# A conditional residual block in fp32r halves: later expert transpose, later layer-0 start, another product order in fc2

## What is computed

```
x = x + (einsum('bsd,bdh->bsh', x, W[cat]) + b[cat])            # 512 -> 512, W[cat] of each entry
h = gelu(einsum('bnd,hd->bnh', x, fc1_w) + fc1_b)               # 512 -> 2048
shared = einsum('bnh,sh->bns', h, fc2_w) + fc2_b                # 2048 -> 384
expert = einsum('bnh,bph->bnp', h, experts_w[e]) + experts_b[e] # 2048 -> 128
x = x + concatenate([shared, expert], axis=-1)
```

## Time and profile before

| what | value |
|---|---|
| median of 3 runs | 1680.94 us (1680.47 to 1681.73) |
| the profiled execution's own time | 1681.4 us |
| its span | 1679.6 us |
| PE busy | 1639.4 us (98%), 7065 matmuls |
| PE weight loads busy | 1315.8 us (78%), beside the matmuls |
| DVE busy | 1176.4 us (70%) |
| ACT busy | 551.9 us (33%) |
| POOL busy | 195.1 us (12%) |
| mean granted PE clock | 0.997 |
| memory traffic | 144 GB/s over the span |

### The profile page before, as it was taken

One profiled execution on the slowest core, in us unless ns is written; L12 is line 12 of the kernel. 1 busy time (PEld: TensorE's weight loads), 2 busy tenths in 40 slices (PEclk: granted clock), 3 DMA queues, 4 the chain that ended last, 5 costly groups with the idle time before them and its releaser, 6 DMA issues.

```text
span 1679.6 us, 28015 instructions
## 1 busy us (share of the span) xinstructions
PE 1639.4 (98%) x7065; PEld 1315.8 (78%) x7065; DVE 1176.4 (70%) x2004; ACT 551.9 (33%) x927; POOL 195.1 (12%) x195
## 2 busy tenths in 40 slices
PE   7899999999999999999999999999999999999999
PEld 5778887877878778787877878778787787878887
DVE  5677667776777767776776677767777677767754
ACT  4343333333323333333332333333333333333321
POOL 0200100111020010200102001110200102001110
PEclk9999999999999999999999999999999999999999
DMA  7886776757677575775767767686775757757630
GB/s 207 185 190 150 147 149 147 156 129 162 127 163 151 131 156 118 167 159 133 149 133 160 156 144 157 131 157 135 163 153 131 155 118 164 163 131 151 134 61 26
DMA packets 884826, 243.44 MB, mean 145 GB/s; under 512 B 803688, under 2 KB 818168, under 8 KB 884732
## 3 DMA queue, kind: packets, MB, share of 16 engines
q1 hardware_dynamic: 740732, 203.75, 57.1%
q10 hardware_dynamic: 144000, 38.82, 10.7%
HBM read 209.93 MB, written 32.51 MB: 144 GB/s over the span
## 4 chain that ended last, share of the span: by engine, by line
PE 66%; SPq 20%; issue 8%; DMA 3%; DVE 2%; ACT 1%; DVEq 0%
PE ps_out L814 30%; PE ps_h L799 14%; PE ps_e L799 13%; PE ps_y L786 8%; SPq L386 8%; SPq L341 4%; SPq L320 2%; DMA e_blocks<-in_L_cond_experts_w 2%; SPq L399 2%; SPq L351 1%; SPq L393 1%; PE ps_t L745 1%; DVE e_whole L643 1%; DVE h L599 1%; DVE w2e L599 1%
## 5 line engine op out<-in xcount | busy, mean ns | idle before, releaser
L814 PE MATMUL ps_out<-w2e,h 128*128 128x512 f32 x3072 | 758.0, 396 | 10.0 <-DVE h L599 10.0
L814 PEld LDWEIGHTS ps_out<-w2e,h 128*128 128x128 f32 x3072 | 574.3, 188 | 152.5 <-DVE h L599 15.9
L799 PE MATMUL ps_e<-y_t,w 128*128 128x512 f32 x1536 | 376.8, 395 | 1.4 <-DVE y_t L599 1.4
L799 PE MATMUL ps_h<-y_t,w 128*128 128x512 f32 x1536 | 375.7, 394 | 0.0
L799 PEld LDWEIGHTS ps_e<-y_t,w 128*128 128x128 f32 x1536 | 290.7, 189 | 66.9 <-DVE y_t L599 1.6
L799 PEld LDWEIGHTS ps_h<-y_t,w 128*128 128x128 f32 x1536 | 288.5, 188 | 65.7
L643 DVE STREAM_TRANSPOSE e_whole<-e_blocks 128x512 f32<-128x512 f32 x256 | 182.0, 711 | 109.3 <-DMA e_blocks<-in_L_cond_experts_w 100.9
L530 ACT CAST w2e<-e_whole 128x512 fp32r<-128x512 f32 x256 | 158.6, 620 | 284.4 <-PE ps_out L814 157.4
L463 POOL TENSOR_TENSOR x_raw<-x_raw,b_all 128x512 f32<-128x512 f32 x60 | 85.3, 1422 | 1354.9 <-DMA x_raw<-in_x 1303.2
L499 ACT CAST w_split<-w_raw 128x512 fp32r<-128x512 f32 x244 | 145.7, 619 | 243.7 <-DMA w_raw<-in_L_cond_W 174.4
L599 DVE TENSOR_TENSOR w_split<-w_raw,w_split 128x512 fp32r<-128x512 f32 x244 | 161.1, 688 | 84.6 <-ACT w_split L499 83.7
(11 more groups left out here) (71 smaller groups left out, 431.3 us busy)
## 6 DMA issues: line engine op xcount, KB each, us to landing
e_blocks<-in_L_cond_experts_w SPq DMA_DIRECT2D x1024, 64.0 KB, 2.9
w_raw<-in_L_cond_W SPq DMA_DIRECT2D x248, 256.0 KB, 2.9
out<-resid SPq DMA_DIRECT2D x64, 256.0 KB, 4.7
x_blocks<-in_x SPq DMA_DIRECT2D x240, 64.0 KB, 2.4
b_all<-in_L_cond_b SPq DMA_DIRECT2D x60, 256.0 KB, 4.3
x_raw<-in_x SPq DMA_DIRECT2D x60, 256.0 KB, 4.6
y_rows<-y ACTq DMA_DIRECT2D x60, 256.0 KB, 2.8
x_blocks<-y_rows ACTq DMA_DIRECT2D x240, 64.0 KB, 3.7
```

The lines of the kernel that those rows point to most:

```text
L799: last = nc.tensor.matmul(h_bank(c)[:, :], w1[:, w, k, c * P:(c + 1) * P], y_t[:, a, k, :, :].rearrange("p b s -> p (b s)"), start=(k == 0 ...
L814: last = nc.tensor.matmul(ps_out[b][:, :], h[:, c % 2, a, b * S:(b + 1) * S], fc2_columns(c, c % 2, w, b), start=(c == 0 and n == 0), stop ...
```

## The change

Five edits, in the order of the diff:

1. L0_STEPS begins with 2 in place of 1: the first two slices of layer 0 for the next group are worked in step 2.
2. In `load_l0_in` everything that belongs to those two slices (two weight slices, the bias, x of entry 0) is issued in step 1 in place of step 0, and the x blocks of entry 1 and the third and fourth slices in step 2 in place of step 1. The x blocks of entry 0 stay in step 0.
3. In SP's step 0 the four stores come behind the expert loads of that step. In group 0 the loads of the two output biases move from step 0 to step 1.
4. On DVE `turn_next_e` stands behind `h_low` in every step, and not in step 0 alone. `turn_x` for entry 0 moves from step 0 to step 1.
5. On PE the three products in fc2 are taken as high-high, low-high, high-low (half of h first), which were high-high, high-low, low-high; and in step 0 of group 0 the first `turn_prep` comes ahead of fc1.

```
-    L0_STEPS = (1, 3, 5, 7, 9, 10, 11, 12)
+    L0_STEPS = (2, 3, 5, 7, 9, 10, 11, 12)
...
-                for b, step in ((0, 0), (1, 1), (2, L0_STEPS[1] + 3), (3, L0_STEPS[3] + 3)):
+                for b, step in ((0, 0), (1, L0_STEPS[0]), (2, L0_STEPS[1] + 3), (3, L0_STEPS[3] + 3)):
                     if c == step:
                         load_x_blocks(G, b)
                 for p in range(2 * GB):
-                    if c == (0 if p == 0 else L0_STEPS[p - 1]):
+                    if c == (L0_STEPS[0] - 1 if p == 0 else L0_STEPS[p - 1]):
...
                 for b in range(GB):
-                    if c == (0 if b == 0 else L0_STEPS[2 * b - 1] + 1):
+                    if c == (L0_STEPS[0] - 1 if b == 0 else L0_STEPS[2 * b - 1] + 1):
                         load_b0(G, b, load_l0_in.cat)
                         load_x(G, b)
...
                     if more:
                         load_l0_in(g + 1, c)
-                    if c == 0 and not first(g):
-                        store(g - 1)
...
                         load_experts(g + 1, quad - NC // QUAD, next_idx, [b])
-                    if first(g) and c == 0:
+                    if c == 0 and not first(g):
+                        store(g - 1)
+                    if first(g) and c == 1:
                         sp.dma_start(b2_all[:, :], fc2_b.rearrange("(o n) -> o n", o=1).to_broadcast([P, SHARED]))\
...
-                    if c > 0:
-                        turn_next_e(g, c, more)
                     h_high(g, c)
                     prep_low(prep_in_step(g, c, 0))
                     h_low(g, c)
-                    if c == 0:
-                        turn_next_e(g, c, more)
+                    turn_next_e(g, c, more)
                     prep_low(prep_in_step(g, c, 1))
                     if more:
-                        if c == 0:
+                        if c == L0_STEPS[0] - 1:
                             turn_x(g + 1, 0)
...
-                    for n, (a, w) in enumerate(((0, 0), (0, 1), (1, 0))):
+                    for n, (a, w) in enumerate(((0, 0), (1, 0), (0, 1))):
                         last = nc.tensor.matmul(ps_out[b][:, :], h[:, c % 2, a, b * S:(b + 1) * S],
...
                 for c in range(NC):
+                    if c == 0:
+                        turn_prep(prep_in_step(g, c, 0))
                     fc1(g, c)
-                    turn_prep(prep_in_step(g, c, 0))
+                    if c > 0:
+                        turn_prep(prep_in_step(g, c, 0))
```

## The result

The changed kernel takes 1740.44 us, the median of 4 runs (1736.18 to 1741.76), against 1681.18 for the kernel before: a ratio of 1.035, 95% interval 1.033 to 1.037. It is slower by 59 us, where 73 were forecast; the time lies inside the range of 1716 to 1767. The profiled execution took 1740.58 us, its span 1738.8.

A forecast was written before the change was run, and what follows sets the result against it. PE bounds the kernel, busy 1639.4 us of a 1679.6 us span. The terms -10 + 53 + 2 + 34 - 6 = +73 us on 1681.4 gave a forecast of 1754 us, range 1716 to 1767.

The forecast's parts named there:

- The chain through SP: SP's queue to layer 0's first slices: 9.7 us delay against 5.6 us room, +53 us in 13 groups, +2 in group 1.
- the eight issues: Four expert blocks and four stores ahead of the first weight slice in SP's queue: 6.3 us of delay.
- the later start of the queue: SP's queue waits for the step-14 expert transpose, now behind h_low, so it starts each next group 3.4 us later.
- The clock: Slow matmuls behind the layer-0 stall at half clock: 2.6 us in each of 13 groups, +34 us.
- the second pair of slices: Third and fourth layer-0 slices, one step behind, meet a late PE: counted 0, up to 0.5 us a group for the range.
- The 10 us at h: fc2's wait for h's low half goes, since h no longer stands behind a waiting expert transpose: -10 us.
- Group 0: The 3.40 us stall in step 3 and its slow clock go: -3.4 - 2.6 = -6 us.
- The order of fc2's products: Same matmuls and weight loads in fc2 in either order: 0, bounded by 6 us either way.
- The faster rival: SP's queue absorbs the delay, layer 0 finds its slices ready, kernel gets faster: 1655 us, chance 0.11.
- the step of 5.6 us: PE reaches layer 0's first slices two blocks later, which gains 5.6 us of room for their transfers.

The follow-up runs named there:

- experiment 1: Changed kernel with the expert transpose ahead of h again in step 14 alone: 1682.93 us.
- experiment 7: Kernel before with the expert transpose behind h in every step but step 14: 1666.03 us, ratio 0.991.
- experiment 10: Kernel before with the expert transpose behind h in step 14 alone (and 0, as before), one run: 1733.04 us.
- experiment 4: Changed kernel with 12 more matmuls, results unread, ahead of PE's wait for the first layer-0 slice in each of 15 groups: 1728.41 us.
- experiment 2: Changed kernel with the expert transpose ahead of h in every step but 0: 1685.66 us.
- experiment 8: Changed kernel with first slices issued in step 0, step-14 expert transpose ahead of h, stores in step 2 behind the second pair of slices: 1653.33 us, ratio 0.984.
- experiment 5: Kernel before with only the expert transpose behind h in every step: 1729.41 us.
- experiment 9: Changed kernel with only the four stores moved, from step 0 to the end of step 1, one run: 1740.58 us.

## Why the prediction was right, and where it was off

- **The chain through SP** held, in sign, place and nearly in size. Forecast: slices 9.7 us later against the first fc1; measured in group 3, 8.9 (12.5 against 3.6). Of this 6.1 us are the eight issues moved ahead: from the first x blocks of the turn to the slices it is 10.0 us (370.94 to 380.97), before 3.9 (361.61 to 365.49). The other 2.8 are the later start of the queue: those x blocks come 2.5 us after the first fc1, before 0.3 us ahead of it. I had 6.3 and 3.4. So the stalls are 4.3 us of wait each and not 5. Experiments 1, 7 and 10 show the step-14 transpose as the cause of the loss; in experiment 1 the eight issues and the later layer 0 together leave the stall at 1.2 us in the mean, where it was 0.8 before the change. For the stalls, with the gains at h and in group 0, the forecast was 53 + 2 - 10 - 3.4 = 42 us; PE's idle time grew by 38.6.
- **The clock** fell as forecast, behind every one of the 14 stalls, group 1's too, where I had not expected it. The term was too large: 34 - 2.6 = 31 us were forecast, and PE's busy time grew by 20.6. The term that was mis-sized is the 2.6 us a group, from one row of before. Measured it is 1.8: from the start of the six matmuls to the fc2 behind them it is 6.01 us in the mean of the 14 groups, and 4.22 before, 25 us together where I had 34. PE's busy time elsewhere fell by the rest, 1.1 us of it in group 0. The six layer-0 matmuls are slow in every group (2.18 to 2.92 us), but the twelve of fc1 behind them take anything from 2.96 to 4.55: 4.02 in group 3, 3.05 in group 1, and 3.4 or less in ten of the 14.
- **What the clock is worth** is another number than what it costs. Experiment 4 gives back only 12 us when it stays up, since the second pair of slices is late as well. The prediction counted 0 for that pair because PE comes late to it; that holds only as long as PE is late.
- **The 10 us at h** went, but I named the wrong cause for this kernel. Experiments 2 and 10 lose them with the transpose ahead of h in that step. The edit wins them where the rest is as before: experiment 7.
- **Group 0** won 3.1 us, not 6: its loop neighbour's first fc1 starts at 155.79, before at 158.88. The stall of 3.40 us is down to 0.45, but the slow clock did not go. It moved two steps on, behind a new stall of 1.88 us, where the six and the twelve matmuls take 2.04 and 4.12 us (before 1.62 and 2.92, after 1.12 us). Why PE stands there was not tried; experiment 8 has a stall of its own in group 0, of 4.36 us.

```profile
82.21 0.63 PE L742 MATMUL ps_t<-ident,prep_raw 128*128 128x128 f32 x4 [1.88 <-issue]
82.60 2.04 PE L783 MATMUL ps_y<-w_split,x_t 128*128 128x512 f32 x6
84.44 4.12 PE L796 MATMUL ps_e<-y_t,w 128*128 128x512 f32 x12
```

- **The order of fc2's products** is worth nothing, as forecast.
- **The faster rival**, that SP absorbs the delay, is out for this order of the queue. It came true in experiment 8, at 1653 us where the rival had 1655: with the step-14 transpose early and the slices ahead of stores and expert blocks the step of 5.6 us is real room. The eight issues cost 6.1 us in this trace. The Trainium skill, "DMA: Bandwidth & Descriptors", section "Anatomy of one DMA — SWDGE (gpsimd) path", lists about 50 ns for a sequencer's dispatch, an estimated 0.4 us for eight; it does so for transfers issued by GpSimd, and the trace of SP's queue disagrees.

## What to carry to other kernels

Before moving an instruction behind another, look for who waits for it on a queue of transfers: the one turn in sixteen that SP's queue waits for sets the start of everything issued after it, and 63 us hung on it here (experiments 5 and 7). A queue has several deadlines one behind the other, so relieving the first shows the second; move the work that nobody waits for (here the stores) behind all of them. And price a stall of PE with the slow matmuls behind it.

## What was not expected of the hardware

The clock fell behind shorter stalls than I had taken from the kernel before, and not by length alone. In experiment 9 six matmuls stayed fast after 3.14 us of idle time (the granted clock is 1.00 from 822.6 to 834 us), and in experiment 4 after 2.62:

```profile
822.53 1.78 PE L783 MATMUL ps_y<-w_split,x_t 128*128 128x512 f32 x6 [3.14 <-DVE w_split L599]
824.15 2.91 PE L796 MATMUL ps_e<-y_t,w 128*128 128x512 f32 x12
```

In experiment 4 they were slow after 1.86 us (2.38), and in experiment 1 after 2.04:

```profile
1397.11 2.19 PE L786 MATMUL ps_y<-w_split,x_t 128*128 128x512 f32 x6 [2.04 <-DVE x_t L599]
1399.09 4.01 PE L799 MATMUL ps_h<-y_t,w 128*128 128x512 f32 x12
```

In experiment 7, after 1.78 us, the six were still fast (1.65) and the twelve behind them slow:

```profile
1377.74 1.65 PE L786 MATMUL ps_y<-w_split,x_t 128*128 128x512 f32 x6 [1.78 <-DVE x_t L599]
1379.23 4.49 PE L799 MATMUL ps_e<-y_t,w 128*128 128x512 f32 x12
```

What besides the length decides is open.
